# Norm factors by ScalarE, six homes for routed rows, and expert outputs summed by adding scatters in DRAM

## The reference

```python
x = layernorm(x + attention(x, Wq, Wk, Wv, Wo, bo))      # 16 heads of 8
x = layernorm(x + retention(x, ctx, ctx))                # 16 heads, decay and rotary factors
x = layernorm(x + ffn(x, gate, w1, w3, w2))              # 8 experts of 512, top 2 per token
# ffn: for the two chosen experts e with softmax weights p_e
#   sum_e p_e * ( (silu(x w1[e]) * (x w3[e])) w2[e] )
# layernorm(v) = (v - mean) / sqrt(var + 1e-5), no gain and no bias
```

## Time and profile before

| what | us |
|---|---|
| median of 3 runs | 1004.99 (1000.88 to 1008.09) |
| profiled execution, its own time | 1007.5 |
| its span in the profile | 1005.7 |
| PE busy | 804.7 (80% of the span) |
| DVE busy | 790.3 (79%) |
| POOL busy | 652.6 (65%) |
| ACT busy | 613.4 (61%) |

### The profile page before, as it was taken

How to read it: one execution, slowest core, us unless ns; L and a number is a source line. 1 busy time by engine, 2 the same in 40 slices (tenths; PEclk the granted TensorE clock), 3 DMA queues, 4 the chain that set the end, 5 groups by cost and what they waited for, 6 DMA issues and landing times.

```text
span 1005.7 us, 34508 instructions
## 1 busy us (share of the span) xinstructions
PE 804.7 (80%) x11940; PEld 603.2 (60%) x11940; DVE 790.3 (79%) x2155; ACT 613.4 (61%) x1416; POOL 652.6 (65%) x738
## 2 busy tenths in 40 slices
PE   1667799989999899898868660999999999999500
PEld 1345465656656556656544430799999999999500
DVE  4797799988999988998846644688888888888475
ACT  1133566768767777676666851676667666766355
POOL 0349767799999999998996456245444544454443
PEclk9788799999999999999987965899999999999855
DMA  9312222123232232221212004222222222222176
GB/s 307 81 29 54 40 48 50 42 62 70 51 71 62 54 74 52 61 58 42 63 39 62 23 22 91 58 61 66 63 62 61 66 63 61 62 65 58 53 252 226
DMA packets 145300, 72.55 MB, mean 72 GB/s; under 512 B 75024, under 2 KB 134544, under 8 KB 145136
## 3 DMA queue, kind: packets, MB, share of 16 engines
q1 hardware_dynamic: 124800, 40.43, 17.4%
q0 software_dynamic: 8640, 17.84, 5.4%
q10 hardware_dynamic: 11696, 12.08, 3.8%
HBM read 41.98 MB, written 28.34 MB: 70 GB/s over the span
## 4 chain that ended last, share of the span: by engine, by line
PE 38%; POOL 32%; issue 12%; DVE 3%; DMA 3%; ACT 2%; POOLq 0%; SPq 0%; ACTq 0%; DVEq 0%
POOL prod_ev L1536 17%; POOL routed_rows L1553 11%; PE QKV L773 9%; PE ST L773 9%; PE XT L801 6%; PE SC L801 5%; POOL rs L1516 3%; PE YY L589 2%; DMA prod_ev<-token_halves 2%; PE SC L560 1%; PE YY L791 1%; PE TR L791 1%; PE TR L606 1%; DMA routed_rows<-xe,pos 1%; PE TR L603 1%
## 5 line engine op out<-in xcount | busy, mean ns | idle before, releaser
L1536 POOL TENSOR_TENSOR prod_ev<-e_sb,q_v 128x512 f32<-128x512 f32 x256 | 300.2, 1206 | 70.5 <-PE YY L589 35.6
L1585 POOL DMA_INDIRECT token_halves<-w_new,tok_i x142 | 137.8, 971 | 32.5 <-issue 22.2
L1553 POOL DMA_INDIRECT routed_rows<-xe,pos x128 | 129.6, 1013 | 30.6 <-issue 29.9
L1151 DVE TENSOR_TENSOR prod_qk<-q_v,QKV 128x2048 f32<-128x2048 f32 x64 | 144.7, 2273 | 4.5 <-ACT q_v L870 4.5
L1438 DVE TENSOR_TENSOR prod_ev<-prod_qk,prod_ev 128x1024 f16<-128x1024 f32 x71 | 87.0, 1226 | 56.0 <-ACT prod_ev L1028 56.0
L1028 ACT CAST prod_ev<-prod_qk 128x1024 f16<-128x1024 f32 x71 | 74.2, 1045 | 76.0 <-DVE prod_qk L1464 51.4
L773 PE MATMUL QKV<-k_t,w_hl 128*128 128x256 f16 x852 | 116.8, 274 | 0.1
L773 PE MATMUL ST<-k_t,w_hl 128*128 128x256 f16 x852 | 116.7, 273 | 0.0
L409 POOL TENSOR_TENSOR marks<-half_c 128x1 f32<-128x1 f32 x103 | 19.9, 193 | 142.2 <-DVE w_new L1454 142.0
L1464 DVE SCALAR_TENSOR_TENSOR prod_qk<-ST,hid_scale,prod_qk 128x512 f32<-128x512 f32 x142 | 99.6, 744 | 2.3 <-ACT prod_qk L1037 2.3
L1037 ACT ACTIVATE prod_qk<-QKV,silu_scale 128x512 f32<-128x512 f32 x142 | 96.1, 678 | 8.6 <-PE QKV L773 4.6
(11 more groups left out here) (169 smaller groups left out, 1695.3 us busy)
## 6 DMA issues: line engine op xcount, KB each, us to landing
w_new<-routed_rows SPq DMA_DIRECT2D x71, 130.0 KB
prod_ev<-token_halves SPq DMA_DIRECT2D x16, 512.0 KB, 5.1
x_sb<-x SPq DMA_DIRECT2D x32, 128.0 KB, 3.0
x_res<-x SPq DMA_DIRECT2D x128, 32.0 KB
head_rows<-o_n SPq DMA_DIRECT2D x32, 128.0 KB
o_t<-head_rows SPq DMA_DIRECT2D x64, 64.0 KB
ctx_sb<-ctx SPq DMA_DIRECT2D x32, 128.0 KB, 2.7
out<-prod_qk ACTq DMA_DIRECT2D x16, 256.0 KB, 4.0
```

The lines of the kernel that those rows point to most:

```text
L1151: eng.tensor_tensor(prod_qk[:, u, :, :].rearrange("p d (i j) -> p d i j", j=NH), q.unsqueeze(3).to_broadcast([P, HD, NH, NH]), k.unsqueeze ...
L1536: ins = eng.tensor_tensor(prod_ev[:, u, q, :, :, 0:HD], e_sb[:, it.slot(2), u, 64 * q:64 * q + 64].rearrange("p (i j) -> p j i", j=4).unsq ...
L1553: eng.indirect_dma_start(out=xs, out_offset=bass.IndirectOffsetOnAxis(ap=pos[:, r, 2 * u + k:2 * u + k + 1], axis=0), in_=xe[:, r, u, k, : ...
L1585: eng.indirect_dma_start(out=halves, out_offset=bass.IndirectOffsetOnAxis(ap=tok_i[:, s, u:u + 1], axis=0), in_=yw[:, s, u, :], in_offset= ...
```

## The change

Four things change.

1. The norm factors of stage A move from POOL to ACT. DVE keeps only `nm`. ACT makes `ve` = ln(var + eps), `rs` = exp(-0.5 ve), and `nb` by four copies with a scale, one for each column; they stand in ACT's step after `row_ids` and ahead of `blocks`. The table set that holds both functions is asked for at the start.
2. `xe` has six homes (`XE_RING`) in place of four.
3. SP also writes the first copy of each normalized duo to `token_sums` in DRAM (4 DMAs of 32 KB per duo, 15 steps late). In stage B `xh` and its addition are gone, `yw` is product * weight, and POOL's scatter adds to `token_sums` in DRAM. Since two tiles can hold the same token, each tile's scatters wait until both scatters of the tile before have landed (`wait_ring(t, half_out, 1, 32)`).
4. Stage C loads one row per token (256 KB per chunk), eight homes instead of four, with no addition; all its steps are unrolled.

```diff
-        halves = nc.dram_tensor("token_halves", [2 * n_tok + 2 * n_exp * TILE, P], F32).ap()
+        token_sums = nc.dram_tensor("token_sums", [n_tok + 2 * n_exp * TILE, P], F32).ap()
@@ SP, stage A
+                if it := at(ROWS_LAG):
+                    r = it.slot(XE_RING)
+                    wait(it, x2_ready)
+                    wait_dma(it, x2_out, 1, 64)
+                    for u in range(2):
+                        for b in range(2):
+                            eng.dma_start(x2_rows[it.number()][u][b], xe[S * u:S * u + S, r, b, 0, 0:P]).then_inc(x2_out, 16)
@@ ACT, stage A
+            def one_over_std(c, d):
+                slot = norm_slot(c, d)
+                wait_norms(c, d, nm_ready)
+                eng.activation(ve[:, slot, :, :], mv[:, slot, :, :, 1], ACT.Ln, bias=eps_c[:, 0:1]).then_inc(ve_ready, 1)
+                wait_norms(c, d, ve_ready)
+                eng.activation(rs[:, slot, :, :].rearrange("p k u -> p (k u)"), ve[:, slot, :, :].rearrange("p k u -> p (k u)"),
+                               ACT.Exp, scale=-0.5).then_inc(rs_ready, 1)
+                wait_norms(c, d, rs_ready)
+                for k in range(2):
+                    for u in range(2):
+                        ins = eng.activation(nb[:, slot, k, u:u + 1], nm[:, slot, k, u:u + 1], ACT.Copy,
+                                             scale=rs[:, slot, k, u:u + 1])
+                ins.then_inc(nb_ready, 1)
@@ ACT, second_norm
-                wait_ring(it, routed_out, RING, 64)
+                wait_row_ring(it, routed_out, XE_RING)
+                wait_dma(it, x2_out, XE_RING, 64)
@@ DVE, variances
-                eng.tensor_scalar(nm[:, slot, :, :], mv[:, slot, :, :, 0], -1.0, None, ALU.mult)
-                eng.tensor_scalar(ve[:, slot, :, :], mv[:, slot, :, :, 1], EPS, None, ALU.add).then_inc(ve_ready, 1)
+                eng.tensor_scalar(nm[:, slot, :, :], mv[:, slot, :, :, 0], -1.0, None, ALU.mult).then_inc(nm_ready, 1)
@@ ACT, stage B
-                    wait_ring(t, xg_in)
-                    wait(t, yw_ready, RING)
-                    eng.mul(xh[:, t.slot(RING), :, :], xg[:, t.slot(RING), :, 0:P], 0.5).then_inc(xh_ready, 1)
@@ DVE, stage B
-                        ins = eng.scalar_tensor_tensor(out=yw[:, s, u, :], in0=YB[t.slot(2)][:, P * u:P * u + P],
-                                                       scalar=wt[:, s, u:u + 1], in1=xh[:, s, u, :], op0=ALU.mult, op1=ALU.add)
+                        ins = eng.tensor_scalar(yw[:, s, u, :], YB[t.slot(2)][:, P * u:P * u + P], wt[:, s, u:u + 1], None, ALU.mult)
@@ POOL, stage B
+                    wait_ring(t, half_out, 1, 32)
                     for u in range(2):
-                        eng.indirect_dma_start(out=halves, ..., in_=yw[:, s, u, :], in_offset=None).then_inc(half_out[s], 16)
+                        eng.indirect_dma_start(out=token_sums, ..., in_=yw[:, s, u, :], in_offset=None, compute_op=ALU.add).then_inc(half_out[s], 16)
@@ DVE, stage C
-                    eng.tensor_tensor(y[:, :, 0, :], y[:, :, 0, :], y[:, :, 1, :], ALU.add).then_inc(fsum_ready, 1)
-                    wait(c, fsum_ready)
```

More of the change, by code:

```diff
@@ L173, in wait_ring, with wait_row_ring @@
     item.eng.wait_ge(sems[(item.off - back) % RING], item.ring_count(per, back))
+def wait_row_ring(item, sems, back):
+    if item.off - back >= 0:
+        item.eng.wait_ge(sems[(item.off - back) % XE_RING], 64 * ((item.off - back) // XE_RING + 1))
 def run_steps(eng, n, first, lags, body):
@@ L377, in build @@
         ev_ready = [sem(f"ev_ready{u}") for u in range(2)]
-        ve_ready, rs_ready = sem("ve_ready"), sem("rs_ready")
-        x_in, ctx_in, routed_out = (ring_sem(n) for n in ("x_in", "ctx_in", "routed_out"))
+        nm_ready, ve_ready, rs_ready = sem("nm_ready"), sem("ve_ready"), sem("rs_ready")
+        x_in, ctx_in = (ring_sem(n) for n in ("x_in", "ctx_in"))
+        routed_out = [sem(f"routed_out{i}") for i in range(XE_RING)]
+        x2_out = sem("x2_out")
         y_in = ring_sem("y_in")
@@ L489, in _ @@
                               pad_rows[:, 2 * n:2 * n + 2, :]).then_inc(blank_out, 16)
-            for r in range(RING):
-                eng.wait_ge(routed_out[r], 64 * n_duo // RING)
+            for r in range(XE_RING):
+                eng.wait_ge(routed_out[r], 64 * ((n_duo - r + XE_RING - 1) // XE_RING))
+            eng.wait_ge(x2_out, 64 * n_duo)
             eng.wait_ge(blank_out, 16 + 16 * n_exp)
@@ L853, in row_ids @@
                 wait(it, w1_ready)
-                eng.copy(xe[:, it.slot(RING), :, :, P + 1],
+                eng.copy(xe[:, it.slot(XE_RING), :, :, P + 1],
                                 const("ids")[:, bass.ds(it.number() * 4, 4)].rearrange("p (u k) -> p u k", k=2)
@@ L979, in step @@
                     row_ids(it)
+                c, d = at(8), at(8 + NORM_GAP)
+                if c or d:
+                    one_over_std(c, d)
                 if it := at(9):
@@ L1449, in tile_step @@
                     wait(t, down_done)
-                    wait(t, xh_ready)
                     wait(t, wt_ready)
@@ L1583, in scatter_tile @@
                     stand(t, 5)
+                    wait_ring(t, half_out, 1, 32)
                     for u in range(2):
-                        eng.indirect_dma_start(out=halves, out_offset=bass.IndirectOffsetOnAxis(ap=tok_i[:, s, u:u + 1], axis=0),
-                                               in_=yw[:, s, u, :], in_offset=None).then_inc(half_out[s], 16)
+                        eng.indirect_dma_start(out=token_sums, out_offset=bass.IndirectOffsetOnAxis(ap=tok_i[:, s, u:u + 1], axis=0),
+                                               in_=yw[:, s, u, :], in_offset=None, compute_op=ALU.add).then_inc(half_out[s], 16)
             run_steps(eng, n_tiles, B_FIRST, B_LAGS, scatter_tile)
```

84 lines of the change are left out of this document (31 added, 53 removed).

## The result

The changed kernel takes 1101.31 us, the median of 4 runs (1093.53 to 1106.11), beside 1006.54 for the kernel before (1000.88 to 1010.2): 1.094 times as long, interval 1.0856 to 1.1023. The forecast was 975 and a range of 960 to 1018. The profiled execution has a span of 1100.5 us, 94.8 more than before.

The account below looks back on a forecast made before the run. POOL was taken to bound stage A, PE stage B, with stage C's DMA engines 73% busy. Terms -18 - 3 + 0 - 9.4 = -30.4 off the 1005.7 us span gave 975; range 960 to 1018.

Parts of the forecast that it names:

- The second: Stage B rival: scatter chain becomes the bound from 1.25 us extra; 1005 to 1030 us near its threshold; chance 0.18.
- Stage B, the price of the adding: Stage B: adding lengthens a tile's scatter round trip by 0.7 us, to 4.26, hidden under PE, so 0.
- the threshold of 0.81: Stage B: the 3.56 us round trip fits PE's 4.37 us tile by 0.81; excess is paid about 70 times.
- The structure of the chain: Stage B: first to second issue 1.29 us, landing 2.22, waking 0.05, chained from tile to tile: 3.56 us before adding.
- The test at the prediction's end: Stage B: an adding scatter's landing, expected about 2.9 us, would overturn the forecast by itself if over 3.5.
- Stage A, norm factors: Stage A: moving them off POOL saves 1.24 us of its work per step; 0.9 x 20 = -18 us.
- the forecast step of 14.85: Stage A, full pipeline: each step takes 14.85 us instead of 15.74, half a microsecond above the lowest possible.
- the floor of 14.3: Stage A: no step goes below 14.3 us, since PE's 14.31 and DVE's 14.03 of busy time stay.
- the third rival: Stage A: ACT's chain is late by what POOL won, steps stay near 15.6 us, 992 in all; chance 0.15.
- Six homes: Stage A: ACT's waits to rewrite `xe` go; -3 us (0 to -5) at the stage's end.
- SP's rows: Stage A: four more DMAs per step, 2.29 us for four, fit into SP's idle time: 0.
- Stage C: Stage C: -1.2 us ahead of the loop, -8.2 from chunks of 2.2 instead of 2.75: -9.4 (bounds -3, -14).

Follow-up runs that it names:

- idle_small_c8: Kernel before with norm factors on ACT, six homes, eight 512 KB homes in stage C, 0.4 us of unused POOL products per step: 968.2 us, 0.963.
- homes_c8: Kernel before with six homes for routed rows and stage C read through eight homes of 512 KB, nothing else changed: 992.8 us, 0.988.
- homes_only: Kernel before with six homes for routed rows alone: 999.2 us, 0.994.
- idle_c8: Kernel before with norm factors on ACT, six homes, an unused power and product on POOL, eight 512 KB homes in stage C: 989.6 us, 0.984.

## Why the prediction was wrong

- **The sum.** Against the forecast the span is 41 us longer by stage A, 89 by stage B and 5 shorter by stage C: 975 + 41 + 89 - 5 = 1100. No single rival has this. The second, with its 0.18, names stage B's part; no one names stage A's.
- **Stage B, the price of the adding** is the step that failed most: "I take 0.7 us, nearer the low end". The extra is 5.45 - 3.56 = 1.9 us, between the bounds of 0 and 2.25, and on the far side of the threshold of 0.81. Three terms were each too low: the landing (+1.1), the scatter's own time on POOL, which I had not let grow at all (1.29 to 1.88, +0.6), and the waking (0.27, where I wrote 0.05; it is the same for a plain scatter that is waited for, so it is no price of the adding). The structure of the chain was right: from 4.35 us a tile to 5.59 over 70 tiles is 86 of the measured 89 us. The threshold was less sharp than I had it, since a plain scatter, well under it, already lost 16 us in one execution. The argument that "the read of the destination shares one issue and one completion with the write and only the access itself is added" has no row behind it: the issue alone grew by 0.6, and the packets, almost three times as many on the queue, show that it is no longer the same transfer. The test at the prediction's end, a landing over 3.5 us, would have been too lenient: 3.3 was enough, and beside an issue of 1.88 and a waking of 0.27 any landing over 4.37 - 2.15 = 2.2 us is enough.
- The two rules of the Trainium skill pointed apart, and both describe a part of it. By the one on an accumulating DMA (DMA: Bandwidth & Descriptors, "Rules for kernel authors") each tenth above the threshold is paid; the trace agrees (1.2 us a tile, 86 of 89 us). By the one on source reads (Collectives: The Full Stack, "The bandwidth ceiling: the fold count and why AG ≠ RS ≠ AR") I had a few tenths added, my own step from a rule on bandwidth; the trace shows 1.1 in the landing alone, so for this transfer it is too little.
- **Stage A, norm factors**: "-18 us". The size was sound and reachable: the forecast step of 14.85 is 14.67 in idle_small_c8, above the floor of 14.3. What failed is the assumption under the sum of busy times, that DVE's 14.03 is a fixed amount: it was 16.8 in the change. DVE's operations have a length that depends on where POOL's runs fall, and taking work off POOL moved them. The trace of before had the sign, in its groups of DVE between 200 and 480 us, two operations of one size and kind:

```profile
L1204 DVE TENSOR_TENSOR xq_a<-x,tab 128x256 f32<-128x256 f32 x18 | 16.2, 903 | 0.0
...
L1191 DVE TENSOR_TENSOR xk_a<-ctx_sb,tab 128x256 f32<-128x256 f32 x18 | 7.5, 417 | 0.0
```

  I read one step of `xq_a`, where it took 0.41. No rival of mine named this; the measured sign of the stage is opposite to the forecast.
- **ACT's chain late** (the third rival) did not come. In the step shown, `xq_a` starts at 388.77 with no idle before it, though a step of 17.2 us gives ACT room. At 14.67 us (idle_small_c8, 200 to 480 us) DVE sat idle 1.1 us in all before 19 of them.
- **Six homes**: forecast -3, within 0 to -5, measured alone -8.9, and -7.2 in homes_c8, whose stage A is the same. How much of it lies inside the full pipeline, which I had put into the 14.85, and how much at its end stays open: the last `m_own` is 4.6 us earlier in homes_only than before, and 0.8 later in homes_c8.
- **SP's rows**: forecast 0, measured 0.1, less than two executions of the same stage differ.
- **Stage C**: forecast -9.4, measured -14.4, at the lower bound (-14). What stands ahead of the loop was half of what came (-1.2 taken, 0.5 for the first load and 0.7 for the addition; measured -1.2 for the load and another -1.1 up to the first shift). The loop was mis-sized more: 1.94 us, not 2.2, which is 3.9 us over 15 chunks. `fve` was short in all of them, so the outputs and loads that share the DMA engines did not hold the loop up. By the rule of the Trainium skill that I set beside it (SBUF — State Buffer, "Who interferes with whom") it was to be 1.9; the trace agrees, with `fve` at 0.20 in every chunk here and at 0.55 in 15 of 16 in idle_c8, which has the addition.

## What to carry to other kernels

Before a wait is put around a round trip through DRAM, add up issue, landing and waking of the operation as it will be, with each term at its upper bound: an unmeasured form of transfer that must fit in a margin of 0.8 us should first be timed by itself, in one run. Where VectorE and GpSimd are both nearly full, compare the durations of operations of the same shape: if they differ, GpSimd's runs may be holding VectorE up, and taking work off either moves the meeting place. Then a cheap shift of the order or of the phase is worth timing before work is moved to another engine, and more than one of them: here 0.4 us of unused work in front of GpSimd's products gained 53 us, and two changes of order lost 10 and 15.

## What was not expected of the hardware

- A scatter with an addition holds GpSimd for 1.57 us in place of 0.98, and the queue that carries it moves the same bytes in 24544 packets in place of 8640.
- A VectorE operation of 0.17 us can take 2.5 us beside a pair of GpSimd's products, and two engines of which one is full and the other waits for its results repeat the meeting in each step: the same stage takes 17.2 or 14.7 us a step for 0.4 us of unused work.
- Two readings stay open: what holds `xk_a` for the 0.6 us before POOL's pair begins, and why an adding scatter's landing is 3.2 to 3.4 us most times and 4.4 to 4.9 in some.
